# Ten instead of eight embedding tables looked up by matrix products, with the start-up and the id loads rearranged

## What is computed

```python
e = jnp.stack([tbl_0[ids[:, 0]], ..., tbl_25[ids[:, 25]]], axis=1)
all_vecs = jnp.concatenate([dense_proj[:, None, :], e], axis=1)
interactions = jnp.einsum('bnd,bmd->bnm', all_vecs, all_vecs)
rows, cols = np.triu_indices(n, k=1)
z = jnp.concatenate([dense_proj, interactions[:, rows, cols]], axis=1)
h = jnp.concatenate([z, r_dense_proj], axis=1)
h = jnp.maximum(h @ W_top1 + b_top1, 0.0)
h = jnp.maximum(h @ W_top2 + b_top2, 0.0)
y = h @ W_top3
```

## Time and profile before

| | us |
|---|---|
| median of 3 runs (413.68 to 417.77) | 415.03 |
| the profiled execution's own time | 416.05 |
| its span, first to last instruction | 414.2 |
| TensorE busy | 339.6 |
| GpSimd busy | 275.3 |
| VectorE busy | 213.2 |
| ScalarE busy | 158.2 |

### The profile page before, as it was taken

One profiled execution on the slowest core, in us unless ns is written; L12 is line 12 of the kernel. 1 busy time (PEld: TensorE's weight loads), 2 busy tenths in 40 slices (PEclk: granted clock), 3 DMA queues, 4 the chain that ended last, 5 costly groups with the idle time before them and its releaser, 6 DMA issues.

```text
span 414.2 us, 13844 instructions
## 1 busy us (share of the span) xinstructions
PE 339.6 (82%) x5888; PEld 296.6 (72%) x5888; DVE 213.2 (51%) x588; ACT 158.2 (38%) x228; POOL 275.3 (66%) x292
## 2 busy tenths in 40 slices
PE   0063669786999799997999899987999898988898
PEld 0063658675888698886888688877888787966776
DVE  1465639694738280927466564828183836521110
ACT  1121246245415361517133642444151814271512
POOL 5777706777777777777777777777777777774000
PEclk9995669999999989998999999996999999998989
DMA  5654834523332527232543524252525233211000
GB/s 84 181 163 158 194 98 73 179 69 101 69 99 62 104 59 103 62 78 81 66 93 71 93 66 94 58 108 57 102 61 81 81 66 99 51 51 43 2 2 0
DMA packets 25248, 34.82 MB, mean 84 GB/s; under 512 B 7995, under 2 KB 19011, under 8 KB 25227
## 3 DMA queue, kind: packets, MB, share of 16 engines
q1 hardware_dynamic: 15995, 15.61, 19.9%
q0 software_dynamic: 9216, 18.89, 17.2%
q10 hardware_dynamic: 16, 0.01, 0.0%
HBM read 34.48 MB, written 0.01 MB: 83 GB/s over the span
## 4 chain that ended last, share of the span: by engine, by line
POOL 30%; PE 24%; DMA 19%; issue 16%; DVE 7%; SPq 2%; ACT 1%; POOLq 0%; DVEq 0%; ACTq 0%
POOL vecs L286 30%; DMA raw<-tbl 11%; PE hid L370 5%; DMA step_ids<-look_ids 4%; DVE onehot L555 4%; PE gram L405 4%; DMA raw<-w_dense 3%; PE vec_dve L330 2%; PE vec_dve L332 2%; PE look_ps L330 2%; PE small L384 2%; PE look_ps L332 2%; PE vec_act L314 1%; DMA vecs<-tbl,ids 1%; DVE gram_rows L533 1%
## 5 line engine op out<-in xcount | busy, mean ns | idle before, releaser
L286 POOL DMA_INDIRECT vecs<-tbl,ids x288 | 275.1, 955 | 103.0 <-issue 85.3
L555 DVE TENSOR_SCALAR onehot<-step_ids,row_no 125x256 fp32r<-125x256 int32 x512 | 158.8, 383 | 122.5 <-DMA step_ids<-look_ids 104.9
L330 PE MATMUL look_ps<-onehot,look_hi 125*128 125x256 f32 x256 | 71.5, 312 | 30.6 <-DVE look_lo L563 20.5
L330 PEld LDWEIGHTS look_ps<-onehot,look_hi 125*128 125x128 f32 x256 | 53.5, 209 | 31.9 <-issue 31.3
L330 PE MATMUL vec_dve<-onehot,look_hi 125*128 125x256 f32 x256 | 69.7, 306 | 7.6 <-ACT looked L668 4.9
L526 ACT COPY vecs_T<-vec_act 128x512 f32<-128x512 f32 x64 | 60.4, 1094 | 24.8 <-PE vec_act L314 24.8
L332 PE MATMUL look_ps<-onehot,look_lo 125*128 125x256 f32 x256 | 68.4, 301 | 0.0
L332 PE MATMUL vec_dve<-onehot,look_lo 125*128 125x256 f32 x256 | 67.0, 296 | 0.0
L405 PE MATMUL gram<-vecs_T 128*27 128x26 f32 x4096 | 54.5, 193 | 15.2 <-issue 11.9
L405 PEld LDWEIGHTS gram<-vecs_T 128*27 128x27 f32 x4096 | 44.9, 104 | 28.1 <-issue 23.0
L330 PEld LDWEIGHTS vec_dve<-onehot,look_hi 125*128 125x128 f32 x256 | 52.7, 206 | 11.5 <-issue 5.4
(11 more groups left out here) (64 smaller groups left out, 232.0 us busy)
## 6 DMA issues: line engine op xcount, KB each, us to landing
step_ids<-look_ids SPq DMA_DIRECT2D x16, 512.0 KB
vecs<-tbl,ids POOLq DMA_INDIRECT x288
raw<-tbl SPq DMA_DIRECT2D x8, 500.0 KB
vecs<-dense SPq DMA_DIRECT2D x16, 64.0 KB
w_sb<-w SPq DMA_DIRECT2D x1, 512.0 KB
raw<-w_dense SPq DMA_DIRECT2D x1, 512.0 KB, 14.0
w_sb<-w_pairs SPq DMA_DIRECT2D x1, 468.0 KB
ids<-ids SPq DMA_DIRECT2D x16, 9.0 KB
```

The costliest lines, as they stand in the source:

```text
L286: nc.gpsimd.indirect_dma_start(out=vecs[j][:, 1 + k, :], out_offset=None, in_=tables[k], in_offset=bass.IndirectOffsetOnAxis(ap=ids_sb[j][ ...
L330: nc.tensor.matmul(bank, look_hi[:, f, ch, :], onehot[:, i % SLOTS, c, :], start=ch == 0, stop=False)
L555: last = nc.vector.tensor_scalar(onehot[:, i % SLOTS, c, :], step_ids[a][0:LOOK_K, f - a * LOOKUPS // 2, :], row_no[0:LOOK_K, ch:ch + 1], ...
```

## The change

Ten tables are looked up and 16 gathered. The step has 10 units instead of 8: five in front of the first Gram part, two between, three behind. PARTS becomes 5, and the first Gram part 12 of 32 groups instead of 16. The mask slots become 5, the raw buffers 3. A table is loaded by two DMAs, of 112 and of 13 partitions. Tile 0 is transposed in the first step instead of the second. On SP the step's ids are loaded ahead of the gathers' ids.

```diff
-LOOKUPS = 8
+LOOKUPS = 10
-RAWS = 4
-SLOTS = 4
+LOAD_K = LOOK_K // 16 * 16
+RAWS = 3
+SLOTS = 5
+HALF_UNITS = LOOKUPS // 2
...
                     if f >= RAWS:
                         sp.wait_ge(table_split, f - RAWS + 1)
-                    sp.dma_start(raw_table(f),
-                                 look_tables[f].rearrange("(p c) d -> p c d", c=LOOK_CH)).then_inc(table_in[f], 16)
+                    src = look_tables[f].rearrange("(p c) d -> p c d", c=LOOK_CH)
+                    for rows in (slice(0, LOAD_K), slice(LOAD_K, LOOK_K)):
+                        sp.dma_start(raw_table(f)[rows], src[rows]).then_inc(table_in[f], 16)
...
                 with sp.Fori(2, pairs) as r:
+                    load_step(2 * r, 0, r)
                     load_ids(2 * r, 0, r)
-                    load_step(2 * r, 0, r)
+                    load_step(2 * r + 1, 1, r)
                     load_dense(2 * r, 0)
                     load_ids(2 * r + 1, 1, r)
-                    load_step(2 * r + 1, 1, r)
                     load_dense(2 * r + 1, 1)
...
-                    for i in range(4):
+                    for i in range(HALF_UNITS):
                         unit(i)
...
                 for i in range(LOOKUPS):
-                    look_up(0, 0, 0, i)
+                    if i == FIRST_TURN:
+                        turn_rows(0, 0, 0, FIRST_TURN // 2)
+                    look_up(0, 0, 0, i, 1 if i >= FIRST_TURN else 0)
                 for i in range(LOOKUPS):
-                    if i == FIRST_TURN:
-                        turn_rows(0, 0, 0, LOOKUPS // 2 + FIRST_TURN // 2)
-                    look_up(1, 1, 0, i, 1 if i >= FIRST_TURN else 0)
+                    look_up(1, 1, 0, i, 1)
...
-                        if s == 1 and i == FIRST_TURN + 2:
+                        if s == 0 and i == FIRST_TURN + 2:
                             copy(0, 0, 0)
...
-                    act.wait_ge(table_in[f], 16)
+                    act.wait_ge(table_in[f], 2 * 16)
...
-                        if s == 1 and i == FIRST_TURN:
+                        if s == 0 and i == FIRST_TURN:
                             copies(0, 0)
```

More of the change, by code:

```diff
@@ L157, in raw_table @@
             return raw[f % RAWS][0:LOOK_K, :].rearrange("p (c d) -> p c d", c=LOOK_CH)
-        w1_dense_raw = raw[0][:, 0:2 * H1].rearrange("p (c n) -> p c n", c=2)
+        w1_dense_raw = raw[LOOKUPS % RAWS][:, 0:2 * H1].rearrange("p (c n) -> p c n", c=2)
         ids_in = [sem(f"ids_in{j}") for j in range(2)]
@@ L252, in _ @@
                     load_table(f)
+                load_step(2, 0, 1)
                 load_ids(2, 0, 1)
-                load_step(2, 0, 1)
                 load_weight(w1_sb[0:CHUNK, 1:3, :], w1_pairs[0:2 * CHUNK, :].rearrange("(c k) n -> k c n", k=CHUNK))
@@ L257, in _ @@
                 load_weight(w1_sb[CHUNK:CHUNK + 1, 3, :], b1)
+                load_step(3, 1, 1)
                 load_dense(2, 0)
                 load_ids(3, 1, 1)
-                load_step(3, 1, 1)
                 load_weight(w2_sb[:, :, :], w2.rearrange("(c k) n -> k c n", k=P))
-                sp.wait_ge(table_split, RAWS + 1)
+                sp.wait_ge(table_split, LOOKUPS - RAWS + 1)
                 sp.dma_start(w1_dense_raw, w1_dense.rearrange("(c k) n -> k c n", k=D)).then_inc(w1_dense_in, 16)
@@ L451, in tile @@
                     last.then_inc(half_gram, 1)
-                    unit(4)
-                    unit(5)
+                    for i in range(HALF_UNITS, HALF_UNITS + 2):
+                        unit(i)
                     if mlp and j == 0:
@@ L457, in tile @@
                         layer3(pair - 1)
-                    unit(6)
-                    unit(7)
+                    for i in range(HALF_UNITS + 2, LOOKUPS):
+                        unit(i)
                     for part in range(PARTS // 2, PARTS):
```

## The result

The changed kernel takes 454.69 us (median of 4 runs, 453.43 to 455.23), the kernel before 415.12 beside it (413.68 to 417.77, 4 runs). The ratio is 1.094, 95% interval 1.088 to 1.100: slower, as forecast, but by 39.6 us where 18 were forecast, and outside the range of 421 to 446. The profiled execution has a span of 451.1 us at a mean clock of 0.936.

What follows compares the result with a forecast made beforehand. GpSimd (45.0 us a pair) and TensorE (42.3) were both taken to bound the loop. Start +1, tile 0 +3.9, tile 1 +1.6, loop +12.1, end -0.3 sum to +18.3 on 416.05: 434.4, 433 as median; range 421 to 446.

Steps and rivals of the forecast that it cites:

- the start: Start up to tile 0's first lookup: 68.2 us against 67.25, +1 (-7 to +8).
- The loop pair: Steady loop: TensorE's pair 42.3 + 3.8 - 0.5 + 0.45 = 46.1 us (45.3 to 47).
- Tile 0 and the end: Tile 0: +3.9 us for 16 more matmuls and a wait for merges; end: -0.3 for fewer transposes.
- the code stays on the chip: Loop: no instruction fetches within it, longer TensorE code priced at nothing; the rival that it no longer stays had 0.05.
- the hole on VectorE: Start: VectorE's masks stand from 35.2 to 43.6, until ScalarE's CAST of table 6 and tile 0's copies are done.
- The first pass, 45.39, also waits for its code; I take it as +3.6: First of the six loop passes: 49.0 us, against 45.39 before.
- the +1.6 for tile 1: Tile 1, 19.88 us before: 1.9 more for lookups less 0.3.
- With the start's traffic I take 27: Start: tile 0's 16th gather, issued at 22.60, lands at 27; 2.5 us is the steady-state landing time.
- Twelve transposes … lead to 29.3: Start: tile 0's transposes on TensorE end at 29.3, then VectorE's copy at 30.4.
- The table loads get no faster: Rival for the start: ten tables at 5.8 us with three buffers, start 79, total 444; chance 0.11.
- The load of table 6: Start: 4.5 us taken, between a gather's 2.5 and the earlier CAST pace of 5.8; its CAST done at 39.5.
- the start runs at VectorE's pace: Rival for the start: the wait around table 6's CAST is covered, ten tables end about 58, total 423; chance 0.17.

Runs made afterwards that it cites:

- eight_all: The changed kernel with 8 tables looked up, 18 gathered, four raw buffers and four mask slots: 398.13 us, ratio to before 0.956.
- late_cast: The changed kernel with ScalarE's CAST of table 6 moved behind tile 0's copies: 445.42 us, beside a before of 418.27.
- fifth_ids: The changed kernel with step loads from the fourth on bringing one table's ids instead of five (results not valid): 432.28 us.
- ten_contig2: The changed kernel with ids laid out so a step's ids are one 5 KB run per partition: 426.13 us, ratio to before 1.028.
- one_load: The changed kernel with each table loaded again in one transfer of 125 partitions: 467.28 us.
- b_split: The kernel before with each table loaded in 112 and 13 partitions, nothing else: 404.05 us, ratio 0.976.
- b_sp2: The kernel before with only SyncE's loads in the changed kernel's order: ratio 1.002, beside a before of 589 us.
- ten_late_contig2: The changed kernel with table 6's CAST behind tile 0's copies and ids in 5 KB runs: 555.68 us, beside a before of 591.
- ten_contig: The changed kernel with a step's ids in one 5 KB run per partition, in another batch: ratio to before 0.949.

## Why the prediction was right and wrong

The direction came out, and the size did not. The step that failed is what the prediction took for tile 1, the first pass and the start. It had +1.6, +3.6 and +1 against the kernel before, and they are +7.9, +8.0 and +8.1; the runs show loads of step ids in 1 KB pieces that hold back TensorE's instructions and tile 0's gathers, and a bank that ScalarE empties late.

- **The loop pair: right.** Forecast 46.1, measured 45.95 to 46.80. Two small misses cancel in it: the base of 42.3 is 42.07 in `eight_all`, and the two tables cost 4.2 where 3.8 were added. VectorE's waits for ids went (104.9 to 22.8 in all, 10.5 of it the start's first wait), though three of 2.40 to 3.75 us are left in tiles 1 to 5, where none over 1 was forecast. GpSimd did not bind.
- **Tile 0 and the end: right** (16.76 for 17.0, 46.57 for 46.25). Also right: the code stays on the chip, and the hole on VectorE with its cause (7.79 for 8.4; shown by `late_cast`).
- **"The first pass, 45.39, also waits for its code; I take it as +3.6", and the +1.6 for tile 1: wrong**, by 4.4 and 6.3 us. I read the first pass's excess as the price of fetching code and scaled it a little. The fetch is cheap; what costs is a fetch that falls into a load of step ids in 1 KB pieces. The change made that load a quarter bigger (512 to 640 KB), and SyncE's new order issues two of them close together, 8 to 9 us apart (96.11 and 104.93, 149.37 and 156.93), where before they come every 22 us (88.36, 110.98, 133.45). How much each of the two does was not told apart. In the kernel before such stops are there as well, in tiles 1 to 3, of 0.86 to 2.53 us, small enough to be passed over. `fifth_ids` and `ten_contig2` take them away with the code unchanged.
- **"With the start's traffic I take 27" for the landing of tile 0's gathers: wrong**, 32. The last gather takes 9.9 us from issue to landing in the place of 2.5, because ids come in small pieces beside it (`ten_contig2`: 2.6 us, landed at 26); loads of the tables in one transfer bring it down in part (`one_load`: there by 29). Next, **"Twelve transposes … lead to 29.3"** lacked a wait: group 2 takes a bank that ScalarE empties behind CASTs of tables still under way, 3.85 us. I had followed ScalarE's order for the `vec_act` bank but not for `vec_dve`. Last, the masks of tile 0's first lookup waited 3.28 us for the ids of the third step, a load I never placed. Together the start was +8.1 over before where +1 (-7 to +8) was forecast; 75.37 is just beyond the upper bound.
- **A rival priced low.** "The table loads get no faster" did not come true, and its price was +11 us over the forecast; `one_load`, where it is true, has a start 15.5 us longer. `b_split`, with nothing but the split, is 2.4% faster than before, and `one_load`'s first CASTs are 5.2 us apart where the change's are 3.2. The load of table 6, which I took as 4.5, took 3.6 (its buffer is free at 43.53, its CAST starts at 47.12), and 5.9 in `one_load`. The rule of the Trainium skill that I weighed for it ("DMA: Bandwidth & Descriptors", Why a DMA increments its semaphore by 16 and not by 1), 16 DMA engines for 112 partitions and five for 125, fits this in direction; my estimate by it, 2.5, was too short. No row shows how many DMA engines took part.
- **A slip.** The rival "the start runs at VectorE's pace" adds 12.6, 36.5, 4 and one lookup (1.9) to about 58; they make 55.
- **The range** was built from the start's and the loop's bounds as if only one of them could miss. Both came out at their upper ends, the start at +8.1 of +8, the loop at +17.2 of +18. Tile 1 and the first pass had a point each and no bounds, and these two were 10.7 of the 18.6 us.

## What to carry to other kernels

A load broadcast in 1 KB pieces is cheap by its bytes and dear to everything else in the queues: lay the source out so that each partition gets one long run, before anything is moved around it. When a change moves or enlarges such a load, look at what is fetched or gathered in the 10 us behind it, small "issue" gaps of before included. And before work is taken off the busiest engine, ask whether the next engine's own time leaves room: here 42.1 beside 45.0 left 3 us a pair, and two tables cost 4.2.

## What the runs showed that was not expected

- TensorE's instructions come late beside a load in small pieces: stops of 8.22 and 6.60 us in the changed kernel, 1.49 at most in the same tiles with 5 KB pieces.
- A 640 KB step load in 5 KB pieces is there at 6.65 us in the start, where in 1 KB pieces it is there at 12.8.
- In three of the five batches the kernel before took 586 to 591 us. TensorE's Gram matmuls were then in pieces, with gaps of mostly 0.4 to 1.2 us (2.3 at most) that the trace puts down to nothing, and the granted clock was lower (0.78 in `b_sp2`, 0.85 in `ten_late_contig2`). One chip had both: a batch with before at 418 and a later one with 589. Their groups in such batches, first of the kernel before with only SyncE's order changed (`b_sp2`), then of `ten_late_contig2`:

```profile
L405 PE MATMUL gram<-vecs_T 128*27 128x26 f32 x4096 | 93.4, 212 | 144.3 <-issue 143.3
```

```profile
L408 PE MATMUL gram<-vecs_T 128*27 128x26 f32 x4096 | 73.5, 204 | 93.1 <-issue 92.0
```

In such a batch ten tables win against before: `ten_late_contig2` has a ratio to before of 0.932 (0.922 to 0.941), the same kernel in an earlier batch 0.944 (0.935 to 0.953), `ten_contig` (the kernel of `ten_contig2`) 0.949 (0.944 to 0.955), and eight tables with the same ids layout 1.000 (0.996 to 1.004). Why the Gram part is cut up there, whether the clock is cause or effect, and why there is less of it with ten tables, was not found out. The order of two versions of one kernel can depend on such a condition, so before has to run in every batch.
